# A block with cross attention: the output product of both halves in three rounded passes, with split head outputs and a split Wo

## The reference

```python
q = (query @ Wq + bq).reshape(b, sq, 16, 64)          # query = layernorm(x)
k = (key @ Wk + bk).reshape(b, sk, 16, 64)            # key = value = ctx
v = (value @ Wv + bv).reshape(b, sk, 16, 64)
scores = jnp.einsum('bqhd,bkhd->bhqk', q, k) / 8
attn = jax.nn.softmax(scores, axis=-1)
out = jnp.einsum('bhqk,bkhd->bqhd', attn, v).reshape(b, sq, 1024)
out = out @ Wo + bo + residual                        # the output product
out = layernorm(out) * ln_gamma + ln_beta             # x1 = x + out
```

## Time and profile before

| what | us |
|---|---|
| median of three runs (2113.31 to 2113.99) | 2113.93 |
| the profiled execution, its own time | 2112.04 |
| span of the profile, first to last instruction | 2110.3 |
| TensorE busy in the span (97%) | 2056.4 |
| its weight loads, beside the matmuls (85%) | 1802.9 |
| VectorE busy (70%) | 1475.3 |
| ScalarE busy (58%) | 1214.7 |
| GpSimd busy (47%) | 991.0 |

### The profile page before, as it was taken

The page is one execution under the profiler, slowest core; times in us unless marked ns, Lnnn a source line. Parts: engine busy times, 40 slices in busy tenths (PEclk is TensorE's granted clock), DMA queues, the critical chain, the costliest instruction groups (busy, mean ns, idle before and its releaser), DMA issues.

```text
span 2110.3 us, 47564 instructions
## 1 busy us (share of the span) xinstructions
PE 2056.4 (97%) x16168; PEld 1802.9 (85%) x16169; DVE 1475.3 (70%) x2626; ACT 1214.7 (58%) x2951; POOL 991.0 (47%) x833
## 2 busy tenths in 40 slices
PE   7999999999999999999999999899998999999997
PEld 6888888888888888888888888688886888888886
DVE  6666667667667667666676576699996877666665
ACT  4656555555655556565555565477774435555553
POOL 5333333333333333343233333488883334777775
PEclk8999999999999999999999999999999999999999
DMA  4001000000010010010000000245533222333332
GB/s 158 11 21 31 20 20 25 18 27 25 10 35 20 15 35 15 20 35 15 20 25 25 20 10 19 94 141 164 167 107 98 90 81 44 56 54 53 55 53 42
DMA packets 99645, 103.89 MB, mean 49 GB/s; under 512 B 10912, under 2 KB 89120, under 8 KB 99584
## 3 DMA queue, kind: packets, MB, share of 16 engines
q1 hardware_dynamic: 85952, 84.47, 12.8%
q0 software_dynamic: 13632, 18.62, 5.5%
HBM read 72.52 MB, written 30.54 MB: 49 GB/s over the span
## 4 chain that ended last, share of the span: by engine, by line
PE 78%; POOL 8%; issue 5%; DVE 4%; DMA 2%; ACT 2%; POOLq 0%; SPq 0%; DVEq 0%; ACTq 0%
PE banks L940 38%; PE banks L1046 5%; PE banks L1059 5%; PE banks L1031 5%; PE banks L995 4%; PE banks L1712 3%; POOL out_dram L2471 3%; POOL r_x L2435 2%; PE banks L2630 2%; PE banks L2310 2%; POOL index L2442 2%; DMA out_dram<-r_y,index 2%; PE banks L1775 1%; PE banks L1734 1%; PE banks L977 1%
## 5 line engine op out<-in xcount | busy, mean ns | idle before, releaser
L451 POOL TENSOR_TENSOR rinv<-rsum,inverse 128x4 f32<-128x4 f32 x112 | 112.8, 1007 | 481.0 <-ACT probs L569 481.0
L940 PE MATMUL banks<-ctxT_hi,qk_hi 128*128 128x256 f32 x1024 | 301.1, 294 | 0.0
L940 PE MATMUL banks<-ctxT_hi,qk_lo 128*128 128x256 f32 x1024 | 289.2, 282 | 0.0
L940 PE MATMUL banks<-ctxT_lo,qk_hi 128*128 128x256 f32 x1024 | 288.6, 282 | 0.0
L569 ACT ACTIVATE probs<-banks,nbias 128x256 f32<-128x256 f32 x512 | 236.3, 486 | 87.9 <-DVE nbias L701 87.9
L576 ACT ACTIVATE pc<-banks 128x512 f32<-128x512 f32 x256 | 155.9, 610 | 223.4 <-PE banks L940 223.4
L661 DVE TENSOR_TENSOR pT_lo<-banks,pT_hi 128x512 fp32r<-128x512 f32 x256 | 164.8, 685 | 115.0 <-ACT pT_hi L528 114.3
L696 DVE TENSOR_REDUCE peak<-banks 128x4 f32<-128x1024 f32 x128 | 156.6, 1224 | 124.2 <-PE banks L940 124.1
L454 POOL TENSOR_TENSOR probs<-probs,rinv 128x1024 f32<-128x1024 f32 x112 | 212.1, 1894 | 20.0 <-POOL rinv L451 20.0
L940 PE MATMUL banks<-pT_hi,ctx_hi 128*128 128x512 f32 x512 | 207.4, 405 | 1.7 <-DVE pT_lo L661 1.7
L940 PE MATMUL banks<-pT_hi,ctx_lo 128*128 128x512 f32 x512 | 201.5, 394 | 0.0
(11 more groups left out here) (276 smaller groups left out, 5832.1 us busy)
## 6 DMA issues: line engine op xcount, KB each, us to landing
ctx_raw<-in_ctx_dram SPq DMA_DIRECT2D x64, 256.0 KB, 2.8
experts_w<-in_L_ffn_We_dram SPq DMA_DIRECT2D x24, 512.0 KB, 4.0
x_in<-in_x_dram SPq DMA_DIRECT2D x16, 256.0 KB, 2.8
x_again<-in_x_dram SPq DMA_DIRECT2D x16, 256.0 KB, 2.9
x_stream<-z SPq DMA_DIRECT2D x16, 256.0 KB, 2.2
s_x<-x_stream SPq DMA_DIRECT2D x32, 128.0 KB, 3.8
s_x_again<-x_stream SPq DMA_DIRECT2D x32, 128.0 KB, 3.2
x_normalised<-s_xl SPq DMA_DIRECT2D x32, 128.0 KB, 1.7
```

The lines of the kernel that those rows point to most:

```text
L451: nc.gpsimd.tensor_tensor(rinv[:, s % 2, :], rsum[:, s % 2, :], inverse[:, :], ALU.pow).then_inc(rinv_done, 1)
L940: last = nc.tensor.matmul(out, a, b, start=(n == 0), stop=(n == 3 * len(pairs) - 1))
```

## The change

- `do_o` multiplies through `exact3`: the head outputs are `oT_hi` and `oT_lo`, Wo is `wo_hi` and `wo_lo`. The two tiles of head outputs now hold one half at a time, four pairs.
- ScalarE writes the upper part of both banks (`v_upper`), the second one behind the step's exponentials. VectorE writes the lower part of both (`v_lower`) and frees both banks.
- Wo is loaded to `wo_raw`, laid where the biases were and where `oT_hi` and `oT_lo` will be; so its load waits for the biases' last readers. GpSimd splits it in group 0 behind step 3. In that group TensorE and ScalarE wait once for the split.
- In step 6 the query product takes banks 2 and 3, the context product 1 and 0, and the probabilities' transposes 2 and 3.
- `x_in`, `xT_hi`, `xT_lo`, `xb` and `xb_low` move to the region of SBUF that the weights of the opening share with the next stage.

```diff
-    ("pc", 5): (0, 3), ("pt", 5): (1, 0), ("v", 1): (1, 0), ("q", 1): (1, 2),
-    ("pc", 6): (3, 0), ("pt", 6): (1, 3), ("pc", 7): (1, 2), ("pt", 7): (7, 3),
+    ("pc", 5): (0, 3), ("pt", 5): (1, 0), ("v", 1): (1, 0), ("q", 1): (2, 3),
+    ("pc", 6): (1, 0), ("pt", 6): (2, 3), ("pc", 7): (1, 2), ("pt", 7): (7, 3),
...
-    oT = sb("oT", [P, HALF, GT])
+    spare = Region(nc, late.at, HALF * D * 4)
+    biases = spare.take("biases", [P, 2, HEADS * DK])
+    spare = Region(nc, late.at, HALF * D * 4)
+    wo_raw = spare.take("wo_raw", [P, HALF, D])
+    oT_hi = sb("oT_hi", [P, PAIRS, GT], F32R)
+    oT_lo = sb("oT_lo", [P, PAIRS, GT], F32R)
...
-                sp.dma_start(wo[:, :, :], t["L0_xattn_Wo"].rearrange("(m p) n -> p m n", p=P)).then_inc(small_in, 16)
+                sp.wait_ge(wqb_done, 1)
+                sp.wait_ge(setup_lo, 2)
+                sp.dma_start(wo_raw[:, :, :], t["L0_xattn_Wo"].rearrange("(m p) n -> p m n", p=P)).then_inc(bq_in, 16)
...
+        def split_wo():
+            pool.wait_ge(bq_in, 32)
+            nc.gpsimd.tensor_copy(wo_hi[:, :, :], wo_raw[:, :, :]).then_inc(wqb_done, 1)
+            pool.wait_ge(wqb_done, 2)
+            nc.gpsimd.tensor_tensor(wo_lo[:, :, :], wo_raw[:, :, :], wo_hi[:, :, :], ALU.subtract).then_inc(wqb_done, 1)
...
+                if g.kind == 0 and s == 3:
+                    split_wo()
...
+        def v_upper(g, half, j):
+
+            bank, _ = wait_filled(act, g, ("v", half, j))
+            for i in range(2):
+                pair = (1 - half) * PAIRS + 2 * j + i
+                last = nc.scalar.activation(oT_hi[:, 2 * j + i, :], bank[:, i * GT:(i + 1) * GT], ACT.Identity,
+                                            bias=bv[:, pair:pair + 1])
+            last.then_inc(hi_done, 1)
...
-                if b == 2 and (g.cur if half else g.prev):
-
-                    bank, free = wait_filled(act, g, ("v", half, 0))
-                    for i in range(2):
-                        pair = (1 - half) * PAIRS + i
-                        last = nc.scalar.activation(oT[:, pair, :], bank[:, i * GT:(i + 1) * GT], ACT.Identity,
-                                                    bias=bv[:, pair:pair + 1])
-                    last.then_inc(free, 1)
+                values = b == 2 and (g.cur if half else g.prev)
+                if values:
+                    if g.kind == 0:
+
+                        act.wait_ge(wqb_done, 3)
+                    v_upper(g, half, 0)
                 if g.cur and s in EXPS_FIRST:
                     exps(g, s)
+                if values:
+                    v_upper(g, half, 1)
...
+        def v_lower(g, half, j):
+
+            k, _ = place(g, ("v", half, j))
+            dve.wait_ge(hi_done, nth_hi(g, ("v", half, j)))
+            for i in range(2):
+                pair = (1 - half) * PAIRS + 2 * j + i
+                last = nc.vector.scalar_tensor_tensor(
+                    out=oT_lo[:, 2 * j + i, :], in0=ring[:, k, i * GT:(i + 1) * GT], scalar=bv[:, pair:pair + 1],
+                    in1=oT_hi[:, 2 * j + i, :], op0=ALU.add, op1=ALU.subtract)
             last.then_inc(freed[k], 1)
...
-                    bank, free = wait_filled(dve, g, ("v", half, 1))
-                    for i in range(2):
-                        pair = (1 - half) * PAIRS + 2 + i
-                        last = nc.vector.tensor_scalar(oT[:, pair, :], bank[:, i * GT:(i + 1) * GT],
-                                                       bv[:, pair:pair + 1], None, ALU.add)
-                    last.then_inc(free, 1)
+                    for j in range(2):
+                        v_lower(g, half, j)
...
+            if g.kind == 0:
+                pe.wait_ge(wqb_done, 3)
             for n in range(TILES):
-                for m in range(first, first + PAIRS):
-                    last = nc.tensor.matmul(bank[:, n * D:(n + 1) * D], oT[:, m, n * P:(n + 1) * P], wo[:, m, :],
-                                            start=(m == first), stop=(m == first + PAIRS - 1))
+                at = slice(n * P, (n + 1) * P)
+                last = exact3(bank[:, n * D:(n + 1) * D],
+                              [((oT_hi[:, i, at], oT_lo[:, i, at]), (wo_hi[:, first + i, :], wo_lo[:, first + i, :]))
+                               for i in range(PAIRS)])
             last.then_inc(done, 1)
```

More of the change, by code:

```diff
@@ L192, in cross_attention @@
     wv = sb("wv", [P, DC, HEADS * DK])
-    wo = sb("wo", [P, HALF, D])
+    wo_hi = sb("wo_hi", [P, HALF, D], F32R)
+    wo_lo = sb("wo_lo", [P, HALF, D], F32R)
     bq = sb("bq", [P, HALF])
@@ L197, in cross_attention @@
     wqb_parts = early.take("wqb_parts", [P, DC, P // HEADS, HEADS], F32R)
-    xb = sb("xb", [P, GT])
-    xb_low = sb("xb_low", [P, GT])
+    xb = early.take("xb", [P, GT])
+    xb_low = early.take("xb_low", [P, GT])
     qbk = sb("qbk", [P, GB, HALF])
@@ L210, in cross_attention @@
     ctxT_lo = sb("ctxT_lo", [P, GB, DC, SK], F32R)
-    x_in = sb("x_in", [P, TILES, D])
+    x_in = early.take("x_in", [P, TILES, D])
     x_again = sb("x_again", [P, TILES, D])
@@ L218, in cross_attention @@
     rstd = sb("rstd", [P, 2, TILES])
-    xT_hi = sb("xT_hi", [P, DC, GT], F32R)
-    xT_lo = sb("xT_lo", [P, DC, GT], F32R)
+    xT_hi = early.take("xT_hi", [P, DC, GT], F32R)
+    xT_lo = early.take("xT_lo", [P, DC, GT], F32R)
     q_hi = early.take("q_hi", [P, PAIRS, GT], F32R)
@@ L238, in cross_attention @@
     wq_raw = wstage[:, 2048:4096].rearrange("p (c n) -> p c n", c=DC)
-    biases = oT[:, :, :].rearrange("p h n -> p (h n)").rearrange("p (i n) -> p i n", i=2)
     products = probs[:, :, :, :].rearrange("p s i k -> p s (i k)")
@@ L282, in cross_attention @@
                   for k in range(BANKS_USED)]
-    SPLIT = ("ctxT", "xT", "fold", "pt", "wk", "q", "qx", "qx0")
+    SPLIT = ("ctxT", "xT", "fold", "pt", "wk", "q", "qx", "qx0", "v")
     hi_turns = Turns(lambda kind: [key for key in ring_order(kind) if key[0] in SPLIT], -1, GROUPS)
@@ L682, in q_lower @@
                     in1=q_hi[:, 2 * m + i, :], op0=ALU.add, op1=ALU.subtract)
+            last.then_inc(freed[k], 1)
+        def v_lower(g, half, j):
[6 more added lines that the diff above has]
+                    in1=oT_hi[:, 2 * j + i, :], op0=ALU.add, op1=ALU.subtract)
             last.then_inc(freed[k], 1)
@@ L838, in vector @@
                     wait_freed(dve, g, ("qbk0",))
-                    dve.wait_ge(small_in, 16 * 6)
+                    dve.wait_ge(small_in, 16 * 5)
                 elif s == 0 and g.cur:
```

## The result

| | kernel before | changed kernel |
|---|---|---|
| median of 6 runs each, us | 2113.96 (2113.02 to 2115.82) | 2098.66 (2095.87 to 2099.32) |
| ratio, 95% interval | | 0.9924 (0.9914 to 0.9935) |
| profiled execution: span, mean clock | 2110.3, 0.993 | 2097.2, 0.992 |
| first output product starts at | 95.19 | 96.12 |
| second output product of group 15 | 1318.45 | 1303.46 |

Faster by 15.3 us, where 23.9 were forecast: the direction right, inside the range of 2084 to 2100, outside the 2086 to 2095 that the forecast had without its rivals, and a third of the gain missing. The first window is that of the earlier trace rows; the two of 30 us behind it are the end of the cross attention and the start of the shared expert's products, first in the changed kernel, then the same work in the kernel before (us; busy PE, PEld, DVE, ACT, POOL; clock; DMA share; GB/s).

A forecast was written before the change was run, and what follows sets the result against it. A gapless TensorE queue was taken to bound the cross attention; 31 halves x 0.77 = 23.9 us off 2112.04 gave 2088.1, 2090.0 as median. Own range 2086 to 2095, with rivals 2084 to 2100.

The forecast's parts named there:

- What bounds the kernel: Cross attention loop: a queue of TensorE instructions without gaps, so a microsecond taken out comes off the end.
- 24 x 0.1195 us: Output product after the change: 24 rounded passes a half at the query product's price, 2.87 us.
- 3.54 us for 16 full passes: Output product of one half before the change, step 7: 16 full-precision passes, 0.221 us each.
- a switch from full-precision to rounded operands: Fold's first pair behind the output product: its extra 0.10 us read as operand change, gone after the change.
- The rival of a quarter pass: Output product: a rounded pass costs a quarter of a full product, 0.111 us, giving 2083.5 us; chance 0.04.
- Step 2's banks: Head outputs' banks at step 2's context product: bank 1 freed 0.77 us before TensorE asks, so no wait.
- Step 6's banks, margin 1.6 us: Step 6: bank 1's twin freed near 660.7, asked for at 662.34; margin 1.6 us.
- Wo's split and load at 0: Group 0: GpSimd's split of at most 7.6 us and the moved 1 MB load cost 0; 5 us kept for the range.
- The rival of VectorE's lower parts held by GpSimd: Steps 2 and 6: lower parts sit out GpSimd's 2.9 us normalisation; 28 us slower, 2142; chance 0.02.
- The last half at 0: Group 16: VectorE about 0.6 us later, shorter product gives 0.67 back; that half counted as 0.
- A microsecond for a shifted gap: End of the stage, partly at 1.2 GHz behind idle time: a shifted gap can cost or give a microsecond.

The follow-up runs named there:

- late roundings: Changed kernel with ScalarE's two roundings of the first half's head outputs both behind step 2's exponentials, instead of one ahead: 2112.47 us, ratio 0.9994 to the kernel before.

## Why the prediction came out as it did

The mechanism and the direction held; one term was too large, and one cover was missing. That the range held is luck in part: the forecast's own range, 2086 to 2095, did not, and the 5 us that bring 2098.66 inside were added for rivals that did not come true.

- **What bounds the kernel**: right. The loop is a TensorE queue, and what left it came off.
- **24 x 0.1195 us**: right, 0.12 us a pass.
- **3.54 us for 16 full passes, and "a switch from full-precision to rounded operands"**: this step failed. The fold's first pair still holds 0.22 us, where I had said 0.12; and 0.09 us more of the step between row heights was hidden in the 3.54, which I spread over 16 passes as 0.221. A full pass is 0.216: in the kernel before, the last two of the 16 passes that start at 216.72 start at 219.74 (rows below), and 14 passes in 3.02 us make 0.216; what the change saves is 16 x 0.216 - 24 x 0.12 = 0.57 us, not 0.77. From product to product the loop gained 0.59 us a half (a group: 81.91 to 80.72 us), so 30 halves gave 17.8. My evidence, that the extra goes away where rounded follows rounded, held for pairs of one height only: two things changed at that place at once.

```profile
216.72 3.61 PE L1059 MATMUL banks<-wo,oT 128*128 128x256 f32 x16
219.74 0.59 PE L1059 MATMUL banks<-wo,oT 128*128 128x256 f32 x2
```

- **The rival of a quarter pass**: fell, as the passes stand 0.12 us apart and not 0.111. The Trainium skill (FP8 and Floating Point Precision, TensorE Precision Notes) has true FP32 as four passes; that three rounded ones cost three quarters is an estimate from that page. The rows give 0.36 of 0.43, five sixths.
- **Step 2's banks**: right, no wait in any inner group; 0.76 us of margin at bank 1 for 0.77 forecast. The late roundings, which put bank 0 back by 2.8 us against 2.2 of margin, show that the margin counts.
- **Step 6's banks, margin 1.6 us**: right in the 15 groups with a next one, wrong in group 15. There is no next query product there, which stands between the head outputs and the context product; the waits of 0.44 and 1.10 us cost 1.85 us (38.25 us from the group's first product to its second, where 36.98 - 0.57 = 36.4 were due). I had worked out one group and multiplied.
- **Wo's split and load at 0**: right for the waits. No TensorE wait comes from them, and the instruction of line 699, now line 734, kept its range (161 to 1673 ns). The rival of VectorE's lower parts held by GpSimd fell: 128 of them took 468 to 485 ns.
- **The last half at 0**: the wait was right, it grew from 0.93 to 1.45 us where 0.6 more was forecast. But it stands ahead of the last product and used up the gain of group 15's second one, which I had counted: from that product to the one of group 16 are 25.29 us before and 25.2 to 26.2 after. At 26.2, and at 25.7 in the first profile, passes ahead of group 16's product already ran at the lower clock.
- **A microsecond for a shifted gap**: too little. From group 16's product to the end, 766.6 us before became 768.0, 768.8 and 767.8, with granted clocks of 0.89 for 0.94 in two stretches. Some 1.0 us of this goes with the longer time at the lower clock in the second stretch. It falls where the shared expert's products begin, and the passes of their first form start over this time (count: duration; first to last start) before, in the changed kernel and with two more passes of 128 rows:

```profile
L2310 PE MATMUL banks<-f_x_hi,f_w_hi x128: 389/393/632, 1595.0 to 1744.1; 128*128 128x512 f32 x128
L2344 PE MATMUL banks<-f_x_hi,f_w_hi x128: 389/393/633, 1580.3 to 1730.4; 128*128 128x512 f32 x128
L2346 PE MATMUL banks<-f_x_hi,f_w_hi x128: 389/393/628, 1591.9 to 1741.0; 128*128 128x512 f32 x128
```

That is 149.1 us (148.5 in the second profile of before), 150.1 and 149.1. The third has the change and, like the two profiles of before, a clock of 0.94 there; in the eight others with the change it is 0.89, and the time 150.0 to 150.3.

The sum of the first pair of profiles: 17.8 (30 halves) - 1.85 (group 15) - 0.9 (opening) - 0.4 (from there to group 16's product) - 1.5 (behind it) = 13.1 us of span, as measured; by medians 15.3, 16.1 and 13.9 in the three sets. Why the clock stays low for longer behind the loop stays open: the code behind the loop is the same, one profile with the change has no more of it near 1600 us than before, eight have, and no run here sets that apart.

## What to carry to other kernels

A price read at one border between two kinds of work holds only for that border: before giving it a cause, find a place where just one of the two things changes. And where a bank's margin is made by work that stands in between, look at the first and last group of the loop, in which that work is missing. Here a bank table with its own entries for the last group added no instruction to the chip's work and took such a wait away, 1.85 us in the profile.

## What the runs showed of the hardware

- Between rounded passes of 128 and of 64 rows the next weight load started only with its matmul, and 0.09 us before and 0.10 us behind the border were paid, in both directions (0.60 us for an inserted pair of 64 rows, 0.25 for one of 128).
- A full-precision pair of 128x256 passes cost 0.43 us and three rounded ones 0.36: the gain of the rounded form is a sixth.
- A TensorE wait cost more than its idle time in the profile: 0.77 us a group for 0.5 written (late roundings), 1.85 for 1.54 (group 15 of the changed kernel).
